# Attention pass of a graph network kernel: rows scaled by the shares straight from PSUM

## The chip, the cores and the metric

The kernel runs on one core of one Trainium2 chip. The metric is the device time of the whole program in microseconds (us). A core has five engines that matter here: TensorE (PE, with its weight load PEld), VectorE (DVE), ScalarE (ACT), GpSimd (POOL) and SyncE (SP, which here only starts DMAs). PE writes to PSUM, a memory of eight banks; everything else lies in SBUF.

## The reference, cut to what matters

The program is two graph layers, each followed by a feed-forward layer. The change touches the second graph layer, a graph attention of 4 heads of 64 columns over 212,500 edges (12,500 nodes), sorted by destination:

```python
xp = (x @ W).reshape(n, H, C)
a_src = jnp.einsum('nhc,hc->nh', xp, att_src)
a_dst = jnp.einsum('nhc,hc->nh', xp, att_dst)
alpha = jax.nn.leaky_relu(a_src[src] + a_dst[dst], negative_slope=0.2)
amax = jax.ops.segment_max(alpha, dst, num_segments=n)
ex = jnp.exp(alpha - amax[dst])
denom = jax.ops.segment_sum(ex, dst, num_segments=n)
w = ex / denom[dst]
msg = xp[src] * w[..., None]
agg = jax.ops.segment_sum(msg, dst, num_segments=n)
```

## The kernel before

The edges are cut into 1664 chunks of 128 edges, and 32 chunks make a batch: 52 batches, run two to a turn of a hardware loop (`body(i, 0)`, `body(i, 1)`), with the batch's parity `b` choosing the buffers. All of it is hand-ordered: each engine has its own instruction list, and semaphores join them.

**POOL** (L1258 to L1285) gathers: `gather` (L1259) is one indirect DMA that POOL prepares from 128 indices in SBUF (`index[:, b, s:s + 1]`) and that brings 128 rows of `xp_table`, each with 256 columns and 8 logits. There are 32 for a batch. Before each group of 4 it waits until the rows that lay in this place two batches earlier have been scaled (`rows_scaled`, L1265).

**ACT** builds the matrices that place edges at nodes (`matrices`, L1295 and L1298), copies the logits of a batch once all 32 gathers of it have landed (`take_logits`, L1303), takes the exponents, and copies what PE has turned (`keep_shares`, L1313 for the 128 shares, L1314 for the 32 old shares) from the PSUM tile `psW` to the SBUF tiles `share` and `old_share`.

**DVE** does two things for each chunk: `scale` (L1548) multiplies the gathered rows by the shares of the 4 heads into `scaled`, and `add` (L1563) adds PE's product into `sums`, with the old share as a factor. Between them, at fixed places of batch n (from `s == 12` to `s == 28`), it does the softmax steps of batch n+1: scans along the edges, small sums, a reciprocal (L1438 to L1543). Both `scale` and the scans read two tensors from SBUF in the kernel before; `add` reads one tensor from SBUF and one from PSUM.

**PE** multiplies each chunk's scaled rows by its matrix (`combine`, L1383) and, between chunks, turns the logits, tops, sums and shares of the next batch (L1342 to L1374): `turn_logits` waits at `s == 9` for the copied logits, so PE, and behind it DVE, stand still there until the next batch has landed. `turn_shares` (L1372, L1374) writes `psW` at `s == 28`.

**SP** brings the next indices when a batch has landed (L1222) and the next edge data when the shares are kept (`share_ready`, L1224).

The eight PSUM banks are four `part` tiles, `psL`, `psR` (turned rows of tops and sums), `psC` (the columns of the carries, 4 elements wide) and `psW`. The first graph layer has a pass of the same build, with its gather in L347 and its sums in L394 (`TENSOR_TENSOR`, one tensor in SBUF and one in PSUM, 128x256).

Of the kernel before, what the change touches and what calls it, by code (L numbers as in the profile page):

```python
# [11 lines left out]
F32 = mybir.dt.float32  # L12
# [6 lines left out]
P = 128  # L19
# [61 lines left out]
def gnn_kernel(nc, a, out):  # L81
# [15 lines left out]
    with ctx:  # L97
# [1027 lines left out]
        with ExitStack() as st:  # L1125
# [9 lines left out]
            apart = at(st, "s8_apart", [P, 2 * GRP, P])  # L1135
            pick = at(st, "s8_pick", [P, 2 * GRP, P])
            scaled = at(st, "s8_scaled", [P, SCALED, D])
            share = at(st, "s8_share", [P, 2, P])
            old_share = at(st, "s8_old_share", [P, 2, BATCH])
            to_node = at(st, "s8_to_node", [P, P])  # L1140
            score = at(st, "s8_score", [P, P + 1])
# [12 lines left out]
            fade_row = at(st, "s8_fade_row", [1, P])  # L1154
            part = [bank(st, f"s8_part{k}", HALVES, P) for k in range(4)]
            psL = bank(st, "s8_psL", 2, P)
            psR = bank(st, "s8_psR", 2, P)
            psC = bank(st, "s8_psC", 2, 2)
            psW = bank(st, "s8_psW", P + BATCH)
            TOPS, SUMS = 0, 1  # L1160
            psB = [part[k].rearrange("p a b -> p (a b)")[:, 0:P] for k in range(2)]
            psS = part[2].rearrange("p a b -> p (a b)")[:, 0:1]
# [12 lines left out]
            top_turned, top_row_done, top_returned, top_carried_done, running_top, node_top = (sem(f"s8_{n}") for n in ("top_turned", "top_row_done", "top_returned", "top_carried_done", "running_top", "node_top"))  # L1175
            below_top, exp_done, weighted, sum_before_done, chunk_sum, faded = (sem(f"s8_{n}") for n in ("below_top", "exp_done", "weighted", "sum_before_done", "chunk_sum", "faded"))
            sum_turned, fade_kept, sum_row_done, sum_returned, sum_scaled, sum_carried_done = (sem(f"s8_{n}") for n in ("sum_turned", "fade_kept", "sum_row_done", "sum_returned", "sum_scaled", "sum_carried_done"))
            running_sum, node_sum, inverse, shared, old_kept, shares_turned, share_ready = (sem(f"s8_{n}") for n in ("running_sum", "node_sum", "inverse", "shared", "old_kept", "shares_turned", "share_ready"))

            spare_halves = [sums[:, 0, 5 * ROW:7 * ROW], sums[:, 1, 0:7 * ROW]]  # L1180
            source, ends = (spare_halves[0][:, k * ROW:(k + 1) * ROW].bitcast(I32) for k in range(2))
# [26 lines left out]
            with nc.Block() as block:  # L1208
                @block.sync
                def _(sp):  # L1210
                    def load_index(n, b):
                        sp.dma_start(index[:, b, :], a["src_chunk"][:, ds(n * BATCH, BATCH)]).then_inc(index_in[b], 16)

                    def load_edges(n, b):
                        for h in range(HEADS):
                            sp.dma_start(edges[h * BATCH:(h + 1) * BATCH, b, :],
                                         edge_rows[ds(n * BATCH, BATCH), :, :].rearrange("s c e -> s (c e)")).then_inc(edges_in[b], 16)
                        sp.dma_start(whole_row[0:1, b, :], whole_rows[ds(n, 1), :]).then_inc(edges_in[b], 16)

                    def follow(i, b):  # L1220

                        sp.wait_ge(gathered[b], LANDED * i + LANDED)  # L1222
                        load_index(2 * i + b + 2, b)
                        sp.wait_ge(share_ready, 2 * (2 * i + b) + 2)  # L1224
                        load_edges(2 * i + b + 2, b)

                    sp.dma_start(tail_index[:, :], a["dst_chunk"][P - 1:P, :].rearrange("o (q j) -> q (o j)", q=P)).then_inc(tail_index_in, 16)
                    load_index(0, 0)
                    load_index(1, 1)
                    sp.dma_start(source[:, :], a["src_row"]).then_inc(rows_in, 16)  # L1230
                    sp.dma_start(ends[:, :], a["dst_row"]).then_inc(rows_in, 16)
                    sp.dma_start(before[:, :], a["dst_before"]).then_inc(rows_in, 16)
                    sp.dma_start(after[:, :], a["dst_after"]).then_inc(rows_in, 16)
                    sp.dma_start(chunk_ends[:, :], a["dst_chunk"]).then_inc(chunks_in, 16)
                    sp.dma_start(chunk_first[:, :], a["dst_chunk"][0:1, :].broadcast_to([P, CHUNKS])).then_inc(chunks_in, 16)
                    sp.dma_start(head_ends[:, :], ends_flat[0:CHUNKS].rearrange("(b s) -> b s", s=BATCH)).then_inc(chunks_in, 16)
                    sp.dma_start(tail_ends[:, :], ends_flat[last_at:last_at + CHUNKS].rearrange("(b s) -> b s", s=BATCH)).then_inc(chunks_in, 16)
                    sp.dma_start(tail_before[:, :], ends_flat[last_at - 1:last_at - 1 + CHUNKS].rearrange("(b s) -> b s", s=BATCH)).then_inc(chunks_in, 16)
                    sp.wait_ge(tail_in, 16 * KR)
                    sp.dma_start(tail_rows[1:CHUNKS + 1, :].rearrange("(q j) h -> q j h", q=P), rows[:, BATCH:BATCH + KR, D + HEADS:EXT]).then_inc(tails_out, 16)  # L1240
                    sp.dma_start(tail_rows[0:1, :], rows[0:1, BATCH, D + HEADS:EXT]).then_inc(tails_out, 16)
                    sp.wait_ge(tails_out, 32)
                    sp.dma_start(tails[:, 1, :], tail_rows[1:CHUNKS + 1, :].rearrange("(b s) h -> b (s h)", s=BATCH)).then_inc(tails_in, 16)
                    sp.dma_start(tails[:, 0, :], tail_rows[0:CHUNKS, :].rearrange("(b s) h -> b (s h)", s=BATCH)).then_inc(tails_in, 16)
                    sp.wait_ge(edges_made, 1)
                    sp.dma_start(edge_rows.rearrange("(q k) c e -> q k c e", k=KR), edge_flags[:, :, :, :]).then_inc(edges_out, 16)
                    sp.wait_ge(joins_ready, 1)
                    sp.dma_start(whole_rows, by_head[:, 3, :, :].rearrange("b h s -> b (h s)")).then_inc(edges_out, 16)
                    sp.wait_ge(edges_out, 32)
                    load_edges(0, 0)  # L1250
                    load_edges(1, 1)
                    with sp.Fori(0, BATCHES // 2 - 1) as i:
                        follow(i, 0)
                        follow(i, 1)
# [33 lines left out]
                def _(act):  # L1288
# [19 lines left out]
                        act.sem_inc(exp_go, 1)  # L1308
                        act.activation(weight[:, :], score[:, :], ACT.Exp).then_inc(exp_done, 1)

                    def keep_shares(n, b):
                        act.wait_ge(shares_turned, n + 1)
                        act.activation(share[:, b, :], psW[:, 0:P], ACT.Copy).then_inc(share_ready, 1)  # L1313
                        act.activation(old_share[:, b, :], psW[:, P:P + BATCH], ACT.Copy).then_inc(share_ready, 1)  # L1314

                    def body(i, b, more=True, most=True):
                        n = 2 * i + b
                        for g in range(BATCH // GRP):
                            if most or g < BATCH // GRP - 2:
                                matrices(n * (BATCH // GRP) + g + 2, g % 2)  # L1320
                            if more and g == 1:
                                take_logits(i + b, 1 - b)
                            if more and g == 4:
                                exponents(n + 1)
                            if more and g == 6:
                                keep_shares(n + 1, 1 - b)

                    act.wait_ge(info_made, 1)
                    matrices(0, 0, False)
                    matrices(1, 1, False)  # L1330
                    take_logits(0, 0)
                    exponents(0)
                    keep_shares(0, 0)
                    with act.Fori(0, BATCHES // 2 - 1) as i:
                        body(i, 0)
                        body(i, 1)
# [4 lines left out]
                def _(pe):  # L1341
# [25 lines left out]
                        pe.transpose(psC[:, SUMS, 0:1], sum_row[0:1, 0:P], ident[0:1, 0:1])  # L1367
                        pe.transpose(psC[:, SUMS, 1:2], sum_row[0:1, BATCH:BATCH + P], ident[0:1, 0:1]).then_inc(sum_returned, 1)

                    def turn_shares(n):  # L1370
                        pe.wait_ge(shared, n + 1)
                        pe.transpose(psW[:, 0:P], spare[:, :], ident[:, :])  # L1372
                        pe.wait_ge(old_kept, n + 1)
                        pe.matmul(psW[:, P:P + BATCH], of_head[:, :], old_part[:, :], start=True, stop=True).then_inc(shares_turned, 1)  # L1374

                    def combine(n, s):
                        c = n * BATCH + s
# [9 lines left out]
                    def body(i, b, more=True):  # L1387
                        n = 2 * i + b
                        for s in range(BATCH):
                            combine(n, s)  # L1390
                            if more and s == 9:
                                turn_logits(n + 1)
                            if more and s == 15:
                                turn_top(n + 1)
                            if more and s == 17:
                                return_top(n + 1)
                            if more and s == 22:
                                turn_sum(n + 1)
                            if more and s == 24:
                                return_sum(n + 1)  # L1400
                            if more and s == 28:
                                turn_shares(n + 1)

                    pe.wait_ge(border_ready, 2)
                    pe.transpose(psB[0][0:1, :], loops[:, ROW - 1:ROW], ident[:, :])
# [15 lines left out]
                    return_top(0)  # L1421
                    turn_sum(0)
                    return_sum(0)
                    turn_shares(0)
                    with pe.Fori(0, BATCHES // 2 - 1) as i:
                        body(i, 0)
                        body(i, 1)
# [4 lines left out]
                def _(v):  # L1432
# [111 lines left out]

                    def scale(n, b, s):
                        if s == 0:
                            v.wait_ge(share_ready, 2 * n + 2)
                        v.tensor_tensor(scaled[:, s % SCALED, :].rearrange("p (k h j) -> p k h j", k=HALVES, h=HEADS),  # L1548
                                        rows[:, b * BATCH + s, 0:D].rearrange("p (k h j) -> p k h j", k=HALVES, h=HEADS),
                                        share[:, b, s::BATCH].unsqueeze(1).unsqueeze(3).broadcast_to([P, HALVES, HEADS, CH // HALVES]),  # L1550
                                        ALU.mult).then_inc(rows_scaled, 1)

                    def nodes(pair):
# [924 lines left out]
```

## Time and profile before

| what | value |
|---|---|
| time, three runs | 6628.99 us median (6628.88 to 6632.55) |
| span of the profiled execution | 6628.2 us, 0.8 us under the median of the runs |
| PE busy | 4704.7 us (71%) |
| DVE busy | 3983.4 us (60%) |
| ACT busy | 1982.2 us (30%) |
| POOL busy | 4262.0 us (64%) |
| gathers of the attention pass, L1259 | 1664, 1654.5 us busy |
| scale, L1548 | 1664, 687.5 us busy |
| add, L1563 | 1666, 793.6 us busy |
| copy of the shares, L1313 | 52, 277 ns each |

A row of the grouped view reads: line, engine, operation, tile written and tiles read, count; then busy time in us and the mean duration of one in ns; then the idle time of the engine just before them and what ended most of it. "issue" stands for waiting that the profile doesn't explain. A duration is the time from an instruction's start to its last write; DVE starts the next instruction before that end, so the distance from one start to the next (its slot, below) is shorter than the duration.

### The profile page before, as it was taken

How to read it: one execution, taken by the hardware profiler on the slowest of the kernel's cores; microseconds unless marked ns; L12 is line 12 of the kernel's file. 1: busy time of each engine (PE TensorE's matmuls, PEld its weight loads, DVE VectorE, ACT ScalarE, POOL GpSimd, SP SyncE). 2: the span in 40 equal slices, each digit the busy share in tenths (PEclk: the TensorE clock that was granted, in tenths of full speed). 3: DMA queues.
4: the chain of work that ended last, by engine and by line, in shares of the span. 5: the costliest groups of instructions: out<-in, count | busy, mean ns of one | idle time of the engine just before them, and what ended most of it. 6: DMA issues, size and time to landing. Idle time of an engine off the chain costs nothing. (4 is left out here: it accounts for less than half of the span.)

```text
span 6628.2 us, 114498 instructions
## 1 busy us (share of the span) xinstructions
PE 4704.7 (71%) x25073; PEld 4033.2 (61%) x25073; DVE 3983.4 (60%) x11854; ACT 1982.2 (30%) x4950; POOL 4262.0 (64%) x4656
## 2 busy tenths in 40 slices
PE   9965555555555558599276777776766767599997
PEld 4445555555555556599265656565655557599996
DVE  5565555555555559522577777777777768644442
ACT  3310000000000006133144444444444434366664
POOL 1257777777777767255677777777777738544443
PEclk9987777777777779699677777767777775599998
DMA  8843333333333339111444444444444435444445
GB/s 313 319 168 105 104 104 104 104 105 105 104 104 104 105 102 306 44 63 63 146 114 113 113 114 113 113 113 113 114 113 113 113 117 181 143 71 72 72 71 129
DMA packets 376353, 810.49 MB, mean 122 GB/s; under 512 B 88803, under 2 KB 234803, under 8 KB 362453
## 3 DMA queue, kind: packets, MB, share of 16 engines
q0 software_dynamic: 209712, 525.20, 30.1%
q1 hardware_dynamic: 138836, 160.68, 7.7%
q10 hardware_dynamic: 27568, 122.44, 5.0%
q14 instruction: 208, 1.70, 0.1%
q8 instruction: 29, 0.48, 0.0%
HBM read 578.58 MB, written 242.27 MB: 124 GB/s over the span
## 5 line engine op out<-in xcount | busy, mean ns | idle before, releaser
L1259 POOL DMA_INDIRECT s_rows<-xp_table,s_index x1664 | 1654.5, 994 | 507.1 <-issue 449.8
L347 POOL DMA_INDIRECT s_rows<-rel_table,s_staged x1664 | 1580.1, 950 | 520.0 <-issue 496.5
L373 PE MATMUL s_part<-s_pick,s_rows 128*128 128x128 f32 x6656 | 1198.0, 354 | 903.5 <-DMA s_rows<-rel_table,s_staged 704.3
L373 PEld LDWEIGHTS s_part<-s_pick,s_rows 128*128 128x128 f32 x6656 | 1109.8, 260 | 992.3 <-DVE s_pick L381 919.0
L1383 PE MATMUL s_part<-s_pick,s_scaled 128*128 128x128 f32 x6656 | 1422.3, 371 | 378.4 <-DVE s_scaled L1548 351.1
L1383 PEld LDWEIGHTS s_part<-s_pick,s_scaled 128*128 128x128 f32 x6656 | 1192.6, 263 | 575.0 <-issue 277.8
L394 DVE TENSOR_TENSOR sums<-sums,s_part 128x256 f32 x1666 | 702.0, 421 | 933.9 <-PE s_part L373 754.8
L1563 DVE SCALAR_TENSOR_TENSOR sums<-sums,s_old_share,s_part 128x256 f32 x1666 | 793.6, 476 | 418.7 <-PE s_part L1383 281.2
L1295 ACT ACTIVATE s_apart<-window,s_local 128x128 f32<-128x128 f32 x1664 | 531.6, 390 | 1148.9 <-PE s_part L1383 1087.9
L1548 DVE TENSOR_TENSOR s_scaled<-s_rows,s_share 128x256 f32<-128x256 f32 x1664 | 687.5, 413 | 74.6 <-issue 73.5
L2291 POOL DMA_INDIRECT sums_out<-s_y,s_ids x212 | 334.0, 1575 | 485.7 <-DVE s_ids L2400 470.7
L381 DVE TENSOR_SCALAR s_pick<-window,s_local,s_weight 128x128 f32<-128x128 f32 x1669 | 635.1, 381 | 14.0 <-issue 0.2
L330 ACT ACTIVATE s_staged<-s_index 128x32 int32 (+1 forms) x52 | 11.8, 229 | 2003.2 <-DMA s_rows<-rel_table,s_staged 1998.1
L2355 PEld LDWEIGHTS s_psG<-s_hT,s_w_now 128*128 128x128 f32 x3392 | 413.4, 192 | 10.9
L2355 PE MATMUL s_psG<-s_hT,s_w_now 128*128 128x128 f32 x3392 | 414.3, 276 | 0.0
L2364 PE MATMUL s_psY<-s_w_now,s_hid 128*128 128x256 f32 x1696 | 401.0, 379 | 0.0
L303 PE MATMUL s_psO<-rel_w,s_hT 128*128 128x512 f32 x784 | 355.2, 596 | 0.5 <-ACT s_hT L270 0.5
L2364 PEld LDWEIGHTS s_psY<-s_w_now,s_hid 128*128 128x128 f32 x1696 | 305.8, 190 | 32.8
L1298 ACT ACTIVATE s_pick<-s_apart,ones 128x512 f32<-128x512 f32 x416 | 300.2, 722 | 13.5
L2320 ACT ACTIVATE s_hid<-s_psG,s_w_now 128x128 f32<-128x128 f32 x848 | 241.7, 368 | 119.3 <-PE s_psG L2355 119.3
L2314 ACT ACTIVATE s_w_now<-exp_w 128x1024 f32 x212 | 224.1, 1057 | 146.0 <-PE s_psY L2364 145.5
L2399 DVE TENSOR_TENSOR s_y<-s_psY,s_b_now 128x256 f32<-128x256 f32 x212 | 89.9, 424 | 285.8 <-PE s_psY L2364 285.8
(357 smaller groups left out, 5486.8 us busy)
## 6 DMA issues: line engine op xcount, KB each, us to landing
rel_table<-s_rows ACTq DMA_DIRECT2D x98, 1024.0 KB
s_rows<-exp_rows SPq DMA_DIRECT2D x212, 132.0 KB, 2.1
s_rows<-rel_table,s_staged POOLq DMA_INDIRECT x1664, 2.7
s_rows<-xp_table,s_index POOLq DMA_INDIRECT x1664
s_edges<-edge_rows SPq DMA_DIRECT2D x208, 80.0 KB
xp_table<-s_xp ACTq DMA_DIRECT2D x49, 264.0 KB, 3.9
s_x<-in_x SPq DMA_DIRECT2D x98, 128.0 KB, 4.2
s_x<-in_x SPq DMA_DIRECT2D x49, 256.0 KB
```

The lines of the kernel that those rows point to most:

```text
L303: mm = pe.matmul(psO[k][:, c * 512:(c + 1) * 512], hT[:, b, k, :], rel_w[:, k, c * 512:(c + 1) * 512], start=True, stop=True)
L347: pool.indirect_dma_start(out=rows[:, s, :], out_offset=None, in_=rel_table[:, :], in_offset=bass.IndirectOffsetOnAxis(ap=staged[:, 2 * s ...
L373: mm = pe.matmul(part[s % PARTS][:, k, :], rows[:, s, k * P:(k + 1) * P], pick[:, s % PICKS, :], start=True, stop=True)
L381: v.tensor_scalar(pick[:, s % PICKS, :], window[:, :], local[:, ds(c, 1)], weight[:, ds(c, 1)], ALU.is_equal, ALU.mult).then_inc(picked, 1)
L394: v.tensor_tensor(sums[:, :, ds(at_node, P)], sums[:, :, ds(at_node, P)], part[s % PARTS][:, :, :], ALU.add).then_inc(added, 1)
L1259: pool.indirect_dma_start(out=rows[:, b * BATCH + s, :], out_offset=None, in_=xp_table[0:NP, :], in_offset=bass.IndirectOffsetOnAxis(ap=in ...
L1295: act.activation(apart[:, half * GRP + j, :], window[:, :], ACT.Abs, bias=local[:, ds(m * GRP + j, 1)]).then_inc(apart_done, 1)
L1383: mm = pe.matmul(part[s % 4][:, k, :], scaled[:, s % SCALED, k * P:(k + 1) * P], pick[:, s % (2 * GRP), :], start=True, stop=True)
L1548: v.tensor_tensor(scaled[:, s % SCALED, :].rearrange("p (k h j) -> p k h j", k=HALVES, h=HEADS), rows[:, b * BATCH + s, 0:D].rearrange("p ...
L1563: v.scalar_tensor_tensor(out=sums[:, :, ds(at_node, P)], in0=sums[:, :, ds(at_node, P)], scalar=old_share[:, b, s:s + 1], in1=part[s % 4], ...
L2355: mm = pe.matmul(psG[b][:, c, :], w1_now[:, b, at_w:at_w + P], hT[:, b, k, :], start=(k == 0), stop=(k == HALVES - 1))
L2364: mm = pe.matmul(psY[b], hid[:, b, c, :], w2_now[:, b, c * D:(c + 1) * D], start=(c == 0), stop=(c == H1 // P - 1))
```

## The change

The SBUF tile `share` goes, and with it the ACT instruction that filled it. `scale` reads the shares from the PSUM tile where PE turned them. As PE turns the shares of the next batch while this batch is still being scaled, `psW` becomes two banks, chosen by the batch's parity. The bank for it comes from `psC`, whose four columns move behind the 256 columns of `psR` into one bank, `psRC`. ACT still copies the old shares, and the semaphore `share_ready` (two counts a batch) becomes `old_ready` (one count a batch), for which DVE waits before the first scale of a batch and SP before the load of edge data.

```diff
-            share = at(st, "s8_share", [P, 2, P])
...
-            psR = bank(st, "s8_psR", 2, P)
-            psC = bank(st, "s8_psC", 2, 2)
-            psW = bank(st, "s8_psW", P + BATCH)
+            psRC = st.enter_context(nc.psum_tensor("s8_psRC", [P, 512], F32))
+            psR = psRC[:, 0:2 * P].rearrange("p (a b) -> p a b", a=2)
+            psC = psRC[:, 2 * P:2 * P + 4].rearrange("p (a b) -> p a b", a=2)
+            psW = [bank(st, f"s8_psW{k}", P + BATCH) for k in range(2)]
...
-                        sp.wait_ge(share_ready, 2 * (2 * i + b) + 2)
+                        sp.wait_ge(old_ready, 2 * i + b + 1)
...
-                    def keep_shares(n, b):
+                    def keep_old_shares(n, b):
                         act.wait_ge(shares_turned, n + 1)
-                        act.activation(share[:, b, :], psW[:, 0:P], ACT.Copy).then_inc(share_ready, 1)
-                        act.activation(old_share[:, b, :], psW[:, P:P + BATCH], ACT.Copy).then_inc(share_ready, 1)
+                        act.activation(old_share[:, b, :], psW[b][:, P:P + BATCH], ACT.Copy).then_inc(old_ready, 1)
...
-                    def turn_shares(n):
+                    def turn_shares(n, b):
                         pe.wait_ge(shared, n + 1)
-                        pe.transpose(psW[:, 0:P], spare[:, :], ident[:, :])
+                        pe.transpose(psW[b][:, 0:P], spare[:, :], ident[:, :])
                         pe.wait_ge(old_kept, n + 1)
-                        pe.matmul(psW[:, P:P + BATCH], of_head[:, :], old_part[:, :], start=True, stop=True).then_inc(shares_turned, 1)
+                        pe.matmul(psW[b][:, P:P + BATCH], of_head[:, :], old_part[:, :], start=True, stop=True).then_inc(shares_turned, 1)
...
                     def scale(n, b, s):
                         if s == 0:
-                            v.wait_ge(share_ready, 2 * n + 2)
+                            v.wait_ge(old_ready, n + 1)
                         v.tensor_tensor(scaled[:, s % SCALED, :].rearrange("p (k h j) -> p k h j", k=HALVES, h=HEADS),
                                         rows[:, b * BATCH + s, 0:D].rearrange("p (k h j) -> p k h j", k=HALVES, h=HEADS),
-                                        share[:, b, s::BATCH].unsqueeze(1).unsqueeze(3).broadcast_to([P, HALVES, HEADS, CH // HALVES]),
+                                        psW[b][:, s:P:BATCH].unsqueeze(1).unsqueeze(3).broadcast_to([P, HALVES, HEADS, CH // HALVES]),
                                         ALU.mult).then_inc(rows_scaled, 1)
```

## Rows read from the trace of the kernel before

**Rows 1.** Busy time by stretch: before, during and after the loop's gathers
```profile
core 0: us, PE busy (x) PEld busy (x) DVE busy (x) ACT busy (x) POOL busy (x), PEclk, DMA share, GB/s
...
3277.40:5366.10 2088.70, 1477.43 (x7040) 1236.07 (x7040) 1592.05 (x4576) 864.85 (x2210) 1597.17 (x1614) 0.73 0.42 113
5366.10:5425.50 59.40, 45.88 (x228) 37.02 (x228) 47.52 (x131) 25.22 (x64) 0.00 (x0) 0.80 0.04 5
```

**Rows 2.** The gather's line: duration min/median/max in ns, first and last start
```profile
L1259 POOL DMA_INDIRECT s_rows<-xp_table,s_index x1664: 946/947/3829, 3204.8 to 5365.1; - x185
...
  issue: 449.8, 1476
  DVE s_scaled L1548: 57.3, 188
```

**Rows 3.** The page's costliest groups: both passes' gathers and the first pass's sums
```profile
L1259 POOL DMA_INDIRECT s_rows<-xp_table,s_index x1664 | 1654.5, 994 | 507.1 <-issue 449.8
L347 POOL DMA_INDIRECT s_rows<-rel_table,s_staged x1664 | 1580.1, 950 | 520.0 <-issue 496.5
...
L394 DVE TENSOR_TENSOR sums<-sums,s_part 128x256 f32 x1666 | 702.0, 421 | 933.9 <-PE s_part L373 754.8
```

**Rows 4.** Timeline: start, duration; gathers that begin beside a scale, first to last
```profile
3278.98 0.42 DVE L1548 TENSOR_TENSOR s_scaled<-s_rows,s_share 128x256 f32<-128x256 f32 x1
3279.10 1.12 POOL L1259 DMA_INDIRECT s_rows<-xp_table,s_index  x1 [0.30 <-issue]
...
4323.83 0.42 DVE L1548 TENSOR_TENSOR s_scaled<-s_rows,s_share 128x256 f32<-128x256 f32 x1
4323.88 1.19 POOL L1259 DMA_INDIRECT s_rows<-xp_table,s_index  x1 [0.30 <-issue]
...
5361.09 0.42 DVE L1548 TENSOR_TENSOR s_scaled<-s_rows,s_share 128x256 f32<-128x256 f32 x1
5361.29 1.03 POOL L1259 DMA_INDIRECT s_rows<-xp_table,s_index  x1 [0.30 <-issue]
```

**Rows 5.** Timeline: a gather that begins beside an add, one beside a scan
```profile
4322.42 0.47 DVE L1563 SCALAR_TENSOR_TENSOR sums<-sums,s_old_share,s_part 128x256 f32 x1
4322.63 0.95 POOL L1259 DMA_INDIRECT s_rows<-xp_table,s_index  x1 [0.30 <-issue]
...
4301.41 0.41 DVE L1488 TENSOR_TENSOR_SCAN s_spare<-s_edges,s_top 128x128 f32<-128x128 f32 x1
4301.46 1.12 POOL L1259 DMA_INDIRECT s_rows<-xp_table,s_index  x1 [0.30 <-issue]
```

**Rows 6.** Timeline of DVE: two scales (their add: rows 5), and the first pass's sum
```profile
4322.09 0.42 DVE L1548 TENSOR_TENSOR s_scaled<-s_rows,s_share 128x256 f32<-128x256 f32 x1
4322.82 0.42 DVE L1548 TENSOR_TENSOR s_scaled<-s_rows,s_share 128x256 f32<-128x256 f32 x1
...
1503.54 0.42 DVE L394 TENSOR_TENSOR sums<-sums,s_part 128x256 f32 x1
1503.87 0.38 DVE L381 TENSOR_SCALAR s_pick<-window,s_local,s_weight 128x128 f32<-128x128 f32 x1
```

**Rows 7.** One line's instructions: a sum of 128 columns with one tensor in PSUM
```profile
L1461 DVE TENSOR_TENSOR s_score<-s_psL,s_to_node x52: 280/283/291, 3264.7 to 5375.6; 128x128 f32<-128x128 f32 x52
```

**Rows 8.** Timeline of DVE: its long stops in one turn of two batches
```profile
4334.81 0.48 DVE L1563 SCALAR_TENSOR_TENSOR sums<-sums,s_old_share,s_part 128x256 f32 x1 [6.27 <-PE s_part L1383]
...
4362.89 0.43 DVE L1548 TENSOR_TENSOR s_scaled<-s_rows,s_share 128x256 f32<-128x256 f32 x1 [3.06 <-issue]
```

**Rows 9.** Instructions of the tile psW, and who waited for whom
```profile
L1313 ACT ACTIVATE s_share<-s_psW x52: 277/277/278, 3277.0 to 5394.4; 128x128 f32<-128x128 f32 x52
L1314 ACT ACTIVATE s_old_share<-s_psW x52: 192/192/193, 3277.2 to 5394.6; 128x32 f32<-128x32 f32 x52
...
  DVE s_scaled L1548: 1.1, 1
```

**Rows 10.** Timeline: one pass of a row and its carry columns through psR and psC
```profile
3266.31 0.41 DVE L1475 TENSOR_TENSOR_SCAN s_top_row<-s_whole_row,s_psR 1x128 f32<-1x128 f32 x1 [0.47 <-PE s_psR L1350]
...
3266.86 0.23 PE L1355 MATMUL s_psC<-ident,s_top_row 1*128 1x1 f32 x1 [0.59 <-DVE s_top_row L1475]
...
3266.96 0.24 PE L1356 MATMUL s_psC<-ident,s_top_row 1*128 1x1 f32 x1
3267.24 0.22 DVE L1479 SCALAR_TENSOR_TENSOR s_top_carried<-s_psC,s_joins,s_top_before 128x1 f32<-128x1 f32 x1 [0.53 <-PE s_psC L1356]
```

More of the change, by code:

```diff
@@ L1177, in gnn_kernel @@
             sum_turned, fade_kept, sum_row_done, sum_returned, sum_scaled, sum_carried_done = (sem(f"s8_{n}") for n in ("sum_turned", "fade_kept", "sum_row_done", "sum_returned", "sum_scaled", "sum_carried_done"))
-            running_sum, node_sum, inverse, shared, old_kept, shares_turned, share_ready = (sem(f"s8_{n}") for n in ("running_sum", "node_sum", "inverse", "shared", "old_kept", "shares_turned", "share_ready"))
+            running_sum, node_sum, inverse, shared, old_kept, shares_turned, old_ready = (sem(f"s8_{n}") for n in ("running_sum", "node_sum", "inverse", "shared", "old_kept", "shares_turned", "old_ready"))
             spare_halves = [sums[:, 0, 5 * ROW:7 * ROW], sums[:, 1, 0:7 * ROW]]
@@ L1325, in body @@
                             if more and g == 6:
-                                keep_shares(n + 1, 1 - b)
+                                keep_old_shares(n + 1, 1 - b)
                     act.wait_ge(info_made, 1)
@@ L1332, in _ @@
                     exponents(0)
-                    keep_shares(0, 0)
+                    keep_old_shares(0, 0)
                     with act.Fori(0, BATCHES // 2 - 1) as i:
@@ L1401, in body @@
                             if more and s == 28:
-                                turn_shares(n + 1)
+                                turn_shares(n + 1, 1 - b)
                     pe.wait_ge(border_ready, 2)
@@ L1423, in _ @@
                     return_sum(0)
-                    turn_shares(0)
+                    turn_shares(0, 0)
                     with pe.Fori(0, BATCHES // 2 - 1) as i:
```

## The prediction

> **What bounds the kernel now.** The change lies in one stage, so the first view is that of busy time by stretch, laid on the attention pass. In the 2088.7 us from the first scale to the last gather POOL starts 1614 gathers and is busy 1597.2 us [rows 1]. What is left is 491.5 us, or 0.3045 us for each gather; in the gather's own line the longer share of this is "issue", and the part put down to DVE is 57.3 us in 188 times, 0.305 us each, the same gap under another name [rows 2]. So POOL never waits for anybody: the stage is a train of gathers, each 0.947 us (the median) and 0.3045 us of gap. Without anything else 1614 of them would take 1614 x 1.2515 = 2019.9 us. The stage takes 68.8 us more, and all of it lies in gathers that last longer than 0.947 us.
>
> DVE is busy 1592 us of 2089, PE less, and DVE has room: in each turn of two batches (64 gathers, 82.8 us) it stands once for some 6 us until the logits of the next batch have landed, 6.27 us in the turn shown, 5.0 to 7.6 us over the 25 turns, 5.9 us on the mean [rows 8]. The stop of 3 us at the loop's end is no room; it comes in every turn whatever POOL does. After the last gather 59.4 us follow without POOL, in which DVE is the busiest by busy time, 47.5 us [rows 1].
>
> **What makes gathers longer.** Here the page has a pair to compare: the mean is 994 ns in this pass and 950 ns in the first graph layer's, with the same count and nearly the same gap [rows 3]. In the timeline I put every longer gather beside what DVE was doing at its start. A gather that begins while a scale runs ends late by a fixed rule: scale until 4324.25, gather from 4323.88, so 0.37 us of overlap, and the gather is 1.19 us, 0.24 us over 0.947: overlap less 0.13 us. The first such pair (until 3279.40, from 3279.10: 0.30, late by 0.17) and the last (until 5361.51, from 5361.29: 0.22, late by 0.08) obey it too; there are 274 of them and their lateness sums to 57.5 us [rows 4]. A scan, also with two tensors from SBUF, does it as well (0.36 us of overlap, late by 0.17), and an add, with one tensor from SBUF and one from PSUM, doesn't: 0.95 us at 0.26 us of overlap [rows 5]. Gathers that meet nothing but an add at their start number 93, with 0.005 us of lateness together. The scans and small sums of the softmax hold the other 11.3 us (68.8 - 57.5). The gather reads its indices from SBUF; what it shares with DVE is, as these rows have it, the way by which DVE fetches a second SBUF tensor.
>
> **The change part by part.**
> - Scale gets its second tensor from PSUM and becomes an instruction of the add's kind, or more exactly of L394's (in0 SBUF, in1 PSUM, TENSOR_TENSOR, 128x256), beside which the first pass's gathers are at 950 ns [rows 3]. It should stop delaying gathers: -57.5 us. At most everything late goes, -68.8 us. At least: the gathers fall into other phases, and one no longer held by a scale can meet a scan. I replayed the train at 1.2515 us a gather against the scans' times of each batch, with the rule above, for shifts of up to 0.6 us either way: 7 to 15 us of lateness stay where 11.3 us are now. So the gain is 54 to 62 us; I take 57.5.
> - The scale's own cost. Its slot is 0.33 us now (start at 4322.09, the add behind it at 4322.42); L394's, with PSUM, is also 0.33 us (1503.54 to 1503.87), and the durations are 0.42 and 421 ns [rows 3, 5, 6]. I take +0. The upper bound from the nearest row of DVE's loop is the add's slot of 0.40 us (4322.42 to 4322.82), which also reads PSUM: +0.07 us [rows 5, 6]. The new read differs from both in one thing that no row shows: it takes single elements 32 columns apart and holds each for 32 columns. Below nothing it isn't, as no PSUM row has a shorter slot at this size.
> - What +0 and +0.07 are worth: POOL's train gets 57.5/25.2 = 2.3 us a turn shorter (1614/64 = 25.2 turns), so DVE's room falls from 5.9 to 3.6 us for 64 scales, 56 ns each. At +0 that covers all. At +0.07 DVE lacks 0.9 us a turn, 23 us in all, and 52 scales after the last gather add 3.6 us: a gain of 31 us is left.
> - The ACT copy of the shares goes: 52 x 277 ns, with 0.18 us between its start and the next one's [rows 9]. DVE waited for what ACT copies once in 52 batches, 1.1 us, before the first batch, where 0.2 us may come off before POOL needs it. Nothing. ACT is busy 865 us of 2089 [rows 1].
> - The waits: SP's and DVE's go from the count of two to one, at the instruction that was the last of the two before. Behind SP's stand only the five loads of edge data for a batch two on. No time.
> - Two banks for psW: PE writes one while DVE reads the other; no wait is added. psR and psC in one bank: PE writes the columns only after DVE has read the row (0.55 us from one start to the other, with a semaphore between), and DVE reads them after both [rows 10]. No instruction of one engine lay beside the other's there, so nothing to gain or lose.
> - The 59.4 us behind the last gather: at +0 unchanged, within 1 us.
>
> Sum: against the profiled span 6628.2 - 57.5 = 6570.7 us; the median of the runs is 0.8 us above that span, so **6571.5 us**.
>
> The Trainium skill bears on this twice. Its page "SBUF — State Buffer", section "Who interferes with whom", has DVE's second SBUF input come through a read port shared with GpSimd, which agrees with the rows; but the same section reports that a tensor_tensor did not stall GpSimd's DMAs in a test, for which it infers that preparing a DMA needs only the write side. By that scale wouldn't delay gathers now and there would be nothing to gain, 6629 us; the 274 late gathers speak against it. Its page "VectorE: DVE Perf Modes", section on the TRN2 errata, gives a Vector instruction 58 cycles of fixed cost with SBUF and 120 with PSUM at 0.96 GHz, an estimate of +65 ns for each scale; the sum would be 6571.5 + 0.6 x 25.2 + 3.4 = 6590 us. L394's slot contradicts it.
>
> **The rivals.**
> 1. *The lateness stays.* What holds the gather is any dense DVE work, or the read from PSUM in this pattern holds it too; or what is taken from the scales is given to the scans. Then nothing moves: 6629 us. For it: scans are late-makers and POOL's read falls at a random phase. Against: 93 gathers beside an add without lateness, and the first pass.
> 2. *The scale's slot grows to the add's.* The gain shrinks as worked out above: 6629 - 31 = 6598 us. For it: the add's slot, with PSUM among its sources. Against: L394's.
> 3. *Slower: reading PSUM in strides.* If every element of the strided, held read took a second cycle, a scale would gain as much as 256 further columns cost: 128x256 takes 421 ns and 128x128 with one tensor in PSUM 283 ns, so 2 x 138 = 276 ns [rows 3, 7]. 64 of them are 17.7 us a turn against 5.9 us of room: 11.8 x 25.2 = 297 us, and 52 x 0.276 = 14 us behind: 6940 us. DVE would be the bound. The point from which the change loses is 5.9/64, some 90 ns a scale. Nothing speaks for it but that no row shows such a read; the strided read from SBUF costs nothing against a dense one (slots 0.33 both) [rows 6].
>
> **How the numbers follow.** A time can be told from no change from 0.2% on, 13 us. Forecast (54 to 62 us off, 6567 to 6575) 0.76; rival 2, or a gain between 15 and 50 us, 0.13; rival 1 0.06; rival 3 0.05. Faster by more than 13 us are the forecast and rival 2: 0.89. Same 0.06, slower 0.05. The range: the phases after the change may also fall better or worse than my replay, down to no lateness at all (6560) on the one side; on the other it takes in most of rival 2, to a slot 0.067 us longer (64 x 0.067 = 4.3 us a turn, 0.7 more than the room, 17 us in all, and 3.5 us behind: 6592).
>
> **What would show it.** The gather's mean falls from 994 to some 954 ns with the median at 947, and no gather beside a scale is over 0.96 us; those beside scans still are. The stretch of 1614 gathers takes 2031 us. The scale's slot stays at 0.33 us with 421 to 424 ns of duration; DVE's stop for the logits is 3 to 5 us once a turn. The gap of 0.30 us stays and POOL waits for nobody. Wrong would be: late gathers beside scales (rival 1), a slot of 0.40 us or more and no stop left (2, 3), or a change in any other stage.

## The result, and the profile after

The kernel after takes 6566.59 us (median, 6564.69 to 6570.1) against 6629.86 us for the kernel before measured beside it: 63.3 us less, a ratio of 0.9906 (95% interval 0.9893 to 0.9919). The profiled execution is the slowest of those four, 6570.1 us with a span of 6568.3 us, 59.9 us under the span before. Lines behind the removed ACT copy have moved up by one: scale is L1547, add L1562.

The costliest groups of the page after (line, engine, operation, count; busy us, mean ns; idle before it):

```profile
L1259 POOL DMA_INDIRECT s_rows<-xp_table,s_index x1664 | 1589.8, 955 | 507.0 <-issue 445.2
L347 POOL DMA_INDIRECT s_rows<-rel_table,s_staged x1664 | 1581.2, 950 | 520.1 <-issue 494.4
```

Its busy time by stretch, from the first scale to the last gather and behind that:

```profile
core 0: us, PE busy (x) PEld busy (x) DVE busy (x) ACT busy (x) POOL busy (x), PEclk, DMA share, GB/s
3277.40:5301.00 2023.60, 1468.64 (x7042) 1226.59 (x7043) 1586.15 (x4574) 854.36 (x2160) 1532.17 (x1613) 0.74 0.43 117
5303.60:5363.00 59.40, 45.88 (x228) 37.03 (x228) 47.44 (x131) 25.06 (x63) 0.00 (x0) 0.80 0.04 5
```

The attention gathers have lost 1654.5 - 1589.8 = 64.7 us, and their mean, 994 ns before [rows 3], is 955 ns, near the first pass's 950. Idle time of POOL before them is 507.0 us, as it was. The stretch from the end of the last gather to the end of the last add is 59.4 us long as before, and each engine's busy time in it agrees within 0.2 us [rows 1]. So the whole gain lies inside the gathers. That the profiled spans differ by 59.9 us and not 64.7 has its place outside: the first attention gather starts at 3207.1 us instead of 3204.8, and what follows the pass takes 2.6 us more, in code that the change doesn't touch.

The timeline after shows the two cases side by side, gathers that start beside a scale and one that starts beside a scan:

```profile
4018.96 0.41 DVE L1547 TENSOR_TENSOR s_scaled<-s_rows,s_psW 128x256 f32<-128x256 f32 x1
4019.18 0.95 POOL L1259 DMA_INDIRECT s_rows<-xp_table,s_index  x1 [0.31 <-issue]
4019.29 0.47 DVE L1562 SCALAR_TENSOR_TENSOR sums<-sums,s_old_share,s_part 128x256 f32 x1
...
4027.92 0.41 DVE L1547 TENSOR_TENSOR s_scaled<-s_rows,s_psW 128x256 f32<-128x256 f32 x1
4027.96 0.95 POOL L1259 DMA_INDIRECT s_rows<-xp_table,s_index  x1 [0.30 <-issue]
...
4755.15 0.42 DVE L1487 TENSOR_TENSOR_SCAN s_spare<-s_edges,s_top 128x128 f32<-128x128 f32 x1
4755.18 1.14 POOL L1259 DMA_INDIRECT s_rows<-xp_table,s_index  x1 [0.30 <-issue]
```

At 0.19 and 0.37 us of overlap a gather beside a scale is on time; the like of it before was 0.24 us late [rows 4]. The scan still makes its gather late by 0.19 us, at 0.39 us of overlap. The scale's slot is 0.33 us (4018.96 to 4019.29).

### The profile page after: what moved, and what is told of

Its sections match the earlier page's. It is cut to its first block and busy times, and to the rows that moved or that the text cites. A ratio compares the mean times of both kernels' runs of the same rounds, so it can differ in the third digit from the quotient of the medians.

```text
span 6568.3 us, 114421 instructions
## 1 busy us (share of the span) xinstructions
PE 4694.1 (71%) x25073; PEld 4021.8 (61%) x25073; DVE 3980.5 (61%) x11854; ACT 1973.9 (30%) x4898; POOL 4199.1 (64%) x4656
## 5 line engine op out<-in xcount | busy, mean ns | idle before, releaser
L1259 POOL DMA_INDIRECT s_rows<-xp_table,s_index x1664 | 1589.8, 955 | 507.0 <-issue 445.2
L394 DVE TENSOR_TENSOR sums<-sums,s_part 128x256 f32 x1666 | 702.8, 422 | 933.7 <-PE s_part L373 754.5
L1562 DVE SCALAR_TENSOR_TENSOR sums<-sums,s_old_share,s_part 128x256 f32 x1666 | 794.8, 477 | 352.9 <-PE s_part L1382 213.2
L1547 DVE TENSOR_TENSOR s_scaled<-s_rows,s_psW 128x256 f32<-128x256 f32 x1664 | 679.7, 408 | 80.3 <-issue 79.3
L381 DVE TENSOR_SCALAR s_pick<-window,s_local,s_weight 128x128 f32<-128x128 f32 x1669 | 636.1, 381 | 13.9 <-issue 0.2
```

Of the source, the lines that this page charges most:

```text
L381: v.tensor_scalar(pick[:, s % PICKS, :], window[:, :], local[:, ds(c, 1)], weight[:, ds(c, 1)], ALU.is_equal, ALU.mult).then_inc(picked, 1)
L394: v.tensor_tensor(sums[:, :, ds(at_node, P)], sums[:, :, ds(at_node, P)], part[s % PARTS][:, :, :], ALU.add).then_inc(added, 1)
L1259: pool.indirect_dma_start(out=rows[:, b * BATCH + s, :], out_offset=None, in_=xp_table[0:NP, :], in_offset=bass.IndirectOffsetOnAxis(ap=in ...
L1562: v.scalar_tensor_tensor(out=sums[:, :, ds(at_node, P)], in0=sums[:, :, ds(at_node, P)], scalar=old_share[:, b, s:s + 1], in1=part[s % 4], ...
```

## The experiments

Two readings are used. The time, against the kernel before on the same chip. And the gathers' own busy time in the trace, which tells lateness apart from everything else: 1664 gathers at 946 ns are 1574 us. Some 10 us above that lie, before and after the change, in the gathers ahead of the first scale: 57.3 us for 50 or 51 of them.

**e1: put the ACT copy back, unread.**

```diff
+            share = at(st, "s8_share", [P, 2, P])
...
+                        sp.wait_ge(old_ready, 2 * (2 * i + b) + 2)
...
+                        act.activation(share[:, b, :], psW[b][:, 0:P], ACT.Copy).then_inc(old_ready, 1)
                         act.activation(old_share[:, b, :], psW[b][:, P:P + BATCH], ACT.Copy).then_inc(old_ready, 1)
...
-                            v.wait_ge(old_ready, n + 1)
+                            v.wait_ge(old_ready, 2 * n + 2)
```

> The kernel after, with the ACT copy of the shares into an SBUF tile put back but read by nobody (DVE waits for both copies, as before the change). Port theory (a gather that reads its indices is held by a DVE instruction that fetches a second tensor from SBUF): same as the kernel after, 6567 us within 5, gathers of 955 ns on the mean. Copy theory (the gain comes from ACT's shorter work or from one wait less): back by some or all of the 63 us, towards 6630.

Measured: 6570.24 us against 6630.83 (ratio 0.9909, interval 0.9892 to 0.9925), gathers 957 ns. The copy and the second count are worth nothing that can be seen.

**e2: all of the change but the source of scale.** As e1, and:

```diff
-                                        psW[b][:, s:P:BATCH].unsqueeze(1)...
+                                        share[:, b, s::BATCH].unsqueeze(1)...
```

> The kernel after with its banks and its order, but scale reads the shares from an SBUF tile that ACT fills. Port theory: back at the time of before, 6630 us within 8, gathers of 994 ns on the mean, late ones beside scales again. Bank theory (the double psW or the shared psRC brings the gain): 6567 us.

Measured: 6629.84 us against 6630.83 (ratio 0.9999, 0.9989 to 1.0008). Its gathers and scales:

```profile
L1260 POOL DMA_INDIRECT s_rows<-xp_table,s_index x1664 | 1650.2, 992 | 507.0 <-issue 458.0
L347 POOL DMA_INDIRECT s_rows<-rel_table,s_staged x1664 | 1581.1, 950 | 520.1 <-issue 494.5
...
L1549 DVE TENSOR_TENSOR s_scaled<-s_rows,s_share 128x256 f32<-128x256 f32 x1664 | 687.2, 413 | 75.2 <-issue 74.1
```

Between e1 and e2 nothing differs but where the scale reads its shares, and that moves the time by 59.6 us and the gathers by 1650.2 - 1592.1 = 58.1 us. The banks alone do nothing.

**e3: half of the scales.** As e1, and the source is `(psW[b][:, s:P:BATCH] if s % 4 < 2 else share[:, b, s::BATCH])`.

> As e1, but two of each four scales (s % 4 of 0 and 1) read PSUM and two read the SBUF copy. Port theory: the lateness goes with the number of scales that read twice from SBUF, so about half of the 63 us is back, 6598 us (6585 to 6612, as phases repeat each batch), and every late gather stands beside a scale of s % 4 of 2 or 3 or a scan. Rival (DVE's density at the gather's start matters, not the source): 6567 or 6630.

Measured: 6609.3 us against 6630.83 (0.9967, 0.9954 to 0.9979); gathers 1630.6 us, 980 ns. Its timeline has both kinds:

```profile
4037.13 0.41 DVE L1549 TENSOR_TENSOR s_scaled<-s_rows,s_psW 128x256 f32<-128x256 f32 x1
4037.19 0.95 POOL L1260 DMA_INDIRECT s_rows<-xp_table,s_index  x1 [0.30 <-issue]
...
4044.64 0.40 DVE L1549 TENSOR_TENSOR s_scaled<-s_rows,s_share 128x256 f32<-128x256 f32 x1
4044.70 1.18 POOL L1260 DMA_INDIRECT s_rows<-xp_table,s_index  x1 [0.30 <-issue]
```

Same kernel, same overlap of 0.34 to 0.35 us, once on time and once 0.23 us late. I went through all gathers of it by the rule of the prediction: 127 are late beside a scale that reads the SBUF copy, 31 us together, and none beside a scale that reads PSUM. Half of the scales keep 31 of the 57.5 us, a little over half. The time lies above the expected 6598 us, inside the range given, because the gathers late beside scans hold more here than in the kernel after: of the 1630.6 - 1589.8 = 40.8 us, some 10 are theirs.

**e4: the operands of scale swapped**, the share in PSUM first, the rows in SBUF second.

> The kernel after with the scale's operands swapped: in0 is the share in PSUM, in1 the rows in SBUF. Port theory in the form 'one SBUF tensor goes by DVE's own way': same as after, 6567 us. In the form 'whatever is in1 and in SBUF goes by the shared way': all of the lateness is back, 6630 us or somewhat less.

Measured: 6570.84 us against 6630.83 (0.991, 0.9893 to 0.9926), gathers 957 ns. What counts for the scale is that only one of its tensors comes from SBUF, not which place it has.

**e5 and e6: the same thing made in the first graph layer's pass.** One more instruction ahead of L394's sum, in e5 with both tensors in SBUF, in e6 with the product in PSUM as the second:

```diff
+                        v.tensor_tensor(extra[:, :, :], window[:, :].unsqueeze(1).broadcast_to([P, HALVES, P]), ident[:, :].unsqueeze(1).broadcast_to([P, HALVES, P]), ALU.add)
                         v.tensor_tensor(sums[:, :, ds(at_node, P)], sums[:, :, ds(at_node, P)],
```

> The kernel after with one more DVE instruction for each of the 1664 chunks of the FIRST graph layer's pass, ahead of its sum: TENSOR_TENSOR 128x256, both tensors in SBUF, result unused. DVE has room there (about 0.62 us of slots in 1.25 us a chunk), so its own length costs nothing. Port theory: the first pass's gathers become late as the attention pass's were, 950 ns rising to 970 to 1050, and the time rises by 30 to 160 us over the kernel after (the phase to the gathers repeats, hence the width). Rival (it is something of the attention pass alone): no change, 6567 us.

> As e5, but the second tensor of the added instruction is the product in PSUM. Port theory: gathers of the first pass stay at 950 ns, 6567 us within 8. Density theory (any dense DVE work holds the gathers): the same rise as e5.

These ran on a chip on which the kernel before takes 7934.94 us, and gathers wait there for other engines, so that the times say little: 7812.47 us for e5 and 7820.66 us for e6 (ratios 0.9856 and 0.9855), not the rise that was expected between them. The duration of a gather is still readable. First e5's group and a pair of its timeline, then e6's:

```profile
L348 POOL DMA_INDIRECT s_rows<-rel_table,s_staged x1664 | 1621.3, 974 | 892.3 <-issue 446.1
...
1000.33 0.42 DVE L395 TENSOR_TENSOR s_extra<-window,ident 128x256 f32<-128x256 f32 x1
1000.52 1.05 POOL L348 DMA_INDIRECT s_rows<-rel_table,s_staged  x1 [0.30 <-issue]
```

```profile
L348 POOL DMA_INDIRECT s_rows<-rel_table,s_staged x1664 | 1577.5, 948 | 944.9 <-issue 426.3
...
1005.12 0.42 DVE L395 TENSOR_TENSOR s_extra<-window,s_part 128x256 f32<-128x256 f32 x1 [0.53 <-PE s_part L374]
1005.17 0.95 POOL L348 DMA_INDIRECT s_rows<-rel_table,s_staged  x1 [0.30 <-PE s_part L374]
```

An instruction of the same size in the same place makes 1664 gathers 43.8 us longer when both its tensors are in SBUF than when one is in PSUM. Gather by gather, by the rule of the prediction, 312 are late beside the added instruction in e5, 39 us together, and none in e6. In e5's pair the overlap of 0.23 us gives 0.10 us of lateness, the scale's rule again. The effect belongs to the pair of engines, not to the attention pass.

**e12: e5 once more**, meant for a chip on which the kernel before takes 6630 us and the first pass is a train of gathers.

> The kernel of e5 once more, where gathers do not wait for rows. e5's trace showed the first pass's gathers late beside the added instruction (974 ns on the mean against 948 ns in e6). Where the kernel before takes 6630 us, port theory: the first pass is a train of gathers too, so its lateness goes into the time, 30 to 160 us over the kernel after: 6600 to 6730 us. Rival: 6567 us.

It met a chip of the other kind again (the kernel before 8091.55 us, e12 7835.17 us, ratio 0.9682). Its first pass repeats e5's lateness:

```profile
L348 POOL DMA_INDIRECT s_rows<-rel_table,s_staged x1664 | 1622.6, 975 | 923.4 <-issue 445.9
```

That this lateness would go into the time of the first pass is thus argued and not measured; in the attention pass e1 and e2 have measured it.

**e7 to e11: how much room DVE has.** One more DVE instruction in the kernel after, at every fourth, second or single chunk: TENSOR_TENSOR 128x128 with one tensor in PSUM.

```diff
                             scale(n, b, s)
+                            if s % 2 == 1:
+                                v.tensor_tensor(extra[:, :], window[:, :], psW[b][:, 0:P], ALU.add)
```

> The kernel after with one more DVE instruction at every fourth chunk of the attention pass (TENSOR_TENSOR 128x128, one tensor in SBUF, one in PSUM, slot 0.20 us, result unused): 3.2 us more DVE work in each turn of two batches against a room of 3.6 us as the prediction has it. POOL-bound theory: within 8 us of the kernel after, 6567 to 6575, the stop for the logits nearly gone. If DVE or PE already shares the bound: +80 us (3.2 x 25.2).

> As e7 at every second chunk: 6.4 us more a turn against 3.6 us of room. The room of the prediction: 2.8 x 25.2 = 71 us in the loop and 5 us behind it, 6643 us (6620 to 6665). If the room is larger, less; if there is none, +161 us and 6733.

> The kernel of e7 once more: e5 to e8 ran on a chip on which the kernel before takes 7935 us and gathers wait for their predecessors' rows, so nothing there was bound by POOL alone. One extra DVE instruction of 0.20 us at every fourth chunk, 3.2 us a turn against a room of 3.6 us. Where the kernel before takes 6630 us: POOL-bound theory 6567 to 6580 (scans meeting other phases may add some us); DVE or PE sharing the bound: about 6647.

> The kernel of e8 once more, 6.4 us more DVE work a turn against 3.6 us of room. Where the kernel before takes 6630 us: 6643 us (6620 to 6665) by the room of the prediction; less if other stops of DVE take up part of it; 6733 if there is no room.

> The kernel after with one more DVE instruction (0.20 us of slot, one tensor in SBUF, one in PSUM, result unused) at EVERY chunk of the attention pass: 12.8 us a turn of two batches. e10's 6.4 us a turn cost 3 us at most, so the room is over the 3.6 us of the prediction; DVE's waits in the loop of the kernel after sum to 331 us without the stop at the loop's end, 13 us a turn. If all of that is room: 6567 to 6585, plus 10 us behind the last gather. If the room ends near 8 us a turn: (12.8 - 8) x 25.2 + 10 = 131 us more, 6700 us, and POOL then waits for scaled rows.

e7 and e8 ran beside e5 and tell nothing of a train: 7743.0 and 7753.68 us against 7934.94. e9 and e10 ran where the kernel before takes 6630.69 us: e9 6572.8 us (0.9914, 0.9898 to 0.9931), inside the expected 6567 to 6580, e10 6569.3 us (0.9908, 0.9891 to 0.9925). e10 was expected at 6643 us. The added 6.4 us of DVE work a turn cost nothing that can be told, in the loop or behind the last gather, where the stretch to the last add is 59.2 us. Where the work went is shown by what DVE waits for in the loop (us in total, times, longest), first in the kernel after, then in e10:

```profile
DVE sums L1562 <- PE s_part L1382: 204.6, 333, 9.1
DVE sums L1562 <- issue: 126.6, 373, 0.7
DVE s_scaled L1547 <- issue: 79.3, 24, 4.0
```

```profile
DVE sums L1563 <- PE s_part L1383: 110.1, 122, 7.7
DVE sums L1563 <- issue: 97.0, 244, 0.7
DVE s_scaled L1548 <- issue: 80.3, 24, 4.0
```

The add's waits fall by 94.5 + 29.6 = 124 us, most of the added 832 x 0.20 = 166 us. Sorted by length in the two traces, about 35 us of this fall are in stops of 1 us and more, above all the stop for the logits, and the rest in the many short waits ahead of an add, while PE ends its product. e11 (every chunk) met the chip on which the kernel before takes 8091.55 us and stands at 7782.57 us; where the room ends on the other chips stays open.

## Why the prediction was right

**The bound.** POOL's train of gathers: right. Its idle time before the gathers is 507.0 us before and after, and the time follows the gathers' busy time in e1 to e4: 6570.2, 6629.8, 6609.3 and 6570.8 us at 1592.1, 1650.2, 1630.6 and 1592.3 us busy.

**The scales' share, -57.5 us.** Right in mechanism and size. e1 and e2 isolate it at 58 to 60 us, e3 about halves it, and in the kernel after no gather is late beside a scale alone. The prediction's wording of the rule is too narrow in two places, though. It speaks of gathers that begin while a scale runs. Of the 274 late ones only 214 do, with 34.0 of the 57.5 us. The other 60, with 23.5 us, begin up to 0.26 us before the scale that makes them late, and among them are the latest of all. Here an add runs at the gather's start and the scale comes after it:

```profile
3646.71 0.46 DVE L1563 SCALAR_TENSOR_TENSOR sums<-sums,s_old_share,s_part 128x256 f32 x1
3646.84 1.49 POOL L1259 DMA_INDIRECT s_rows<-xp_table,s_index  x1 [0.30 <-issue]
...
3647.10 0.41 DVE L1548 TENSOR_TENSOR s_scaled<-s_rows,s_share 128x256 f32<-128x256 f32 x1
```

The lateness, 0.54 us, is again the time from the gather's start to the scale's end (3647.51) less 0.13 us. Most scales that start so soon after a gather don't make it late; what tells the two kinds apart stays open. The second place: a DVE instruction with one tensor from SBUF can hold a gather too. L381, a TENSOR_SCALAR of the first pass (start 514.60, until 514.94), has only `window` as a tensor of 128x128 (its two other sources are one column each), and the gather that begins beside it at 514.75 is 0.06 us late by the same rule:

```profile
514.60 0.34 DVE L381 TENSOR_SCALAR s_pick<-window,s_local,s_weight 128x128 f32<-128x128 f32 x1
514.75 1.01 POOL L347 DMA_INDIRECT s_rows<-rel_table,s_staged  x1 [0.30 <-issue]
```

In the first pass of the kernel before there are 150 of these, 6.2 us together. They account for most of what its mean of 950 ns is above 946. So the count of SBUF tensors decides for the scale, as e1 to e4 show, but not for every kind of instruction. The prediction's last step, that the two engines share the way of DVE's second SBUF tensor and that it is the gather's read of its indices that is held, fits these rows and stays an inference: every gather here reads its indices from SBUF, and no run changed that.

**What stays beside scans.** I kept the 11.3 us of before in the sum and gave 7 to 15 us from the replay. In the stretch after, 1613 gathers x 0.947 us are 1527.5 us of the 1532.2 us busy: 4.7 us stay. This term was 6.6 us too high, and with it the forecast of 6571.5 us against 6566.6. Two things in the replay can have made it too high, and no run parts them. It used the scale's rule for the scans, overlap less 0.13 us, while the scan's own pairs show less: 0.17 us late at 0.36 [rows 5] and 0.19 at 0.39, so overlap less some 0.2 us. And it took the scans' times from the kernel before; in the kernel after they fall at other phases of the train. How far the phases can swing is seen in e3, where some 15 us stay beside scans and small sums.

**The scale's own cost, +0.** Right. The median distance from a scale's start to the next DVE instruction is 0.336 us in the kernel before and 0.330 in the kernel after. Its durations (minimum, median, maximum) are shown best by e3, which has both kinds in one kernel:

```profile
L1549 DVE TENSOR_TENSOR s_scaled<-s_rows,s_psW x832: 355/411/422, 3279.6 to 5398.5; 128x256 f32<-128x256 f32 x167
L1549 DVE TENSOR_TENSOR s_scaled<-s_rows,s_share x832: 395/417/481, 3281.9 to 5400.2; 128x256 f32<-128x256 f32 x167
```

PSUM, read in single elements 32 columns apart and each held for 32, costs 6 ns less by the median. The 421 to 424 ns that the prediction named as a sign didn't come: the mean in the kernel after is 408. Rival 3 has no ground, nor has rival 2: L394's slot was the right row, the add's was not. The estimate of +65 ns after the Trainium skill's page "VectorE: DVE Perf Modes" (section on the TRN2 errata) isn't borne out by these rows, which show no cost of PSUM at all for this instruction.

**DVE's room, 3.6 us a turn after the change.** Right for the stop, wrong for the room, with no harm to the forecast. The stop for the logits fell from some 6 us a turn on the mean to 3.4 (1.7 to 5.6), close to the 3.6 worked out. The step that failed is the one that counted only this stop as room. The short waits ahead of each add are slack too: e10 put 6.4 us into a turn at no cost, and 2.2 us of the stop were still left. With it the prices of rivals 2 and 3 were too high. By e10, a scale 0.07 us longer (4.5 us a turn) would have cost next to nothing, where I worked out 26 us, and the point from which the change loses (rival 3) would lie at 100 ns a scale or beyond instead of 90. These two are estimates: e10 added an instruction behind every second scale, and no run made the scale itself longer.

**Rival 1, the lateness stays.** Refuted by e1 to e4. Its third form, that the scans take over what the scales let go, hardly shows: what is late beside scans and small sums is some 12 us in the kernel before, 15 in e3 and under 5 in the kernel after. The rule by which it was a rival, from the Trainium skill's page "SBUF — State Buffer", section "Who interferes with whom" (a tensor_tensor did not stall GpSimd's DMAs), doesn't hold for indirect gathers here: e5 and e6 show 26 ns a gather between two tensors from SBUF and one. The same section's other sentence, that a DVE instruction with two SBUF inputs contends with a GpSimd instruction that reads SBUF, agrees with e1 to e6.

**The copy, the waits, the banks, the end.** All at nothing, as e1, e2 and the 59.4 us show.

## What to carry to other kernels

When an engine that is always busy has a median well under its mean, put each long instruction beside what the other engines did at its start: here that one comparison named the cause and its sum before anything was changed. Look also at instructions that start shortly after it. If GpSimd prepares indirect gathers back to back, let the elementwise instructions that DVE runs beside it take one of their two tensors from PSUM where it lies there anyway; the copy to SBUF was no service to DVE (the scale is as fast from PSUM), and reading it cost POOL 58 us, while making it cost nothing (e1). Count an engine's room by all its waits on others, not by its longest one, or better by adding work to it.

## What the runs showed of the hardware that was not expected

The hold works in both directions. A scale that starts within 0.05 us of a gather's start, on either side, can itself be drawn out. In the kernel before, 99 scales last longer than 425 ns, up to 492, and 95 of them start so. With one tensor in PSUM none lasts longer than 423 ns. The same shows in e3: 481 ns at most for the scales from SBUF, 422 for those from PSUM. A scale that starts later in a gather isn't drawn out, so the gather doesn't hold DVE for its whole 0.95 us.

Chips differ. On two of them the kernel before takes 7934.94 and 8091.55 us, and every variant run there gained more against it than the kernel after did elsewhere (ratios 0.9625 to 0.9856 against 0.9906), though all have work added. The attention gathers last nearly as long there (962 ns in e7, 966 in e11, 955 in the kernel after), but they wait: 714.3 us for scaled rows in e11, against gaps of 0.3 us elsewhere.

```profile
L1260 POOL DMA_INDIRECT s_rows<-xp_table,s_index x1664 | 1607.5, 966 | 1192.3 <-DVE s_scaled L1548 714.3
```

DVE has 153 stops of 2 us and more ahead of an add in e11's loop, and 24 in the kernel after. Their cause is open. Whether the change itself is worth more on such a chip is open too, since the kernel after wasn't run on one and no trace of the kernel before was taken there.
